# Identity products where TensorE waits, and VectorE work reordered, at the end of a fused attention before an expert-choice layer

## The reference, cut to what matters

```python
x = x + tanh(g_xattn) * xattn(layernorm(x), ctx, mask, Wq..bo)   # x: 2 x 2048 x 512, ctx: 2 x 77 x 512, one head
x = x + tanh(g_ffn) * ffn(layernorm(x), gate_w, w1, w2)

def ffn(x, gate_w, w1, w2):                 # 8 experts, w1 8 x 512 x 2048, w2 8 x 2048 x 512
    probs = softmax(einsum('ntd,ed->nte', x, gate_w))
    g, m = top_k(probs.transpose(0, 2, 1), 512)      # each expert takes 512 tokens of each batch
    h = gelu(einsum('nekd,edf->nekf', x[batch, m], w1))
    h = einsum('nekf,efd->nekd', h, w2)
    out[batch, m] += g * h
```

## Time and profile before

| | |
|---|---|
| median of 3 runs | 1557.32 us (1556.76 to 1558.54) |
| the profiled execution, its own time | 1556.92 us |
| its span | 1555.2 us |
| TensorE products busy | 1498.2 us, 96% |
| VectorE busy | 1016.6 us, 65% |
| ScalarE busy | 721.5 us, 46% |
| GpSimd busy | 589.4 us, 38% |
| granted TensorE clock, mean | 0.986 |

### The profile page before, as it was taken

The page is one execution under the profiler, slowest core; times in us unless marked ns, Lnnn a source line. Parts: engine busy times, 40 slices in busy tenths (PEclk is TensorE's granted clock), DMA queues, the critical chain, the costliest instruction groups (busy, mean ns, idle before and its releaser), DMA issues.

```text
span 1555.2 us, 20287 instructions
## 1 busy us (share of the span) xinstructions
PE 1498.2 (96%) x7329; PEld 1230.2 (79%) x7329; DVE 1016.6 (65%) x1714; ACT 721.5 (46%) x1270; POOL 589.4 (38%) x554
## 2 busy tenths in 40 slices
PE   6987699999999999999999999999999999999997
PEld 6765477787788888888888888888888888888886
DVE  2677676657766676676667666667667665766543
ACT  2244433355444554454445554554445444554432
POOL 2264555534544044323443244404432344323311
PEclk9998799999999999999999999999999999999999
DMA  7274623533342333344233423334324423342133
GB/s 230 76 242 158 203 89 118 135 127 85 86 123 58 105 88 102 95 88 116 82 109 73 117 78 113 66 97 101 96 89 88 116 81 109 79 111 73 49 71 79
DMA packets 101385, 163.37 MB, mean 105 GB/s; under 512 B 7411, under 2 KB 45315, under 8 KB 101285
## 3 DMA queue, kind: packets, MB, share of 16 engines
q1 hardware_dynamic: 86885, 128.50, 26.5%
q0 software_dynamic: 14400, 33.56, 11.5%
HBM read 128.48 MB, written 33.55 MB: 104 GB/s over the span
## 4 chain that ended last, share of the span: by engine, by line
PE 88%; DVE 7%; DMA 2%; issue 1%; ACT 1%; POOL 1%; SPq 0%; POOLq 0%; DVEq 0%; ACTq 0%
PE bank L1408 42%; PE bank L1294 33%; PE bank L1268 4%; PE bank L1585 2%; PE bank L565 1%; DVE atleast L971 1%; DVE onehot L1468 1%; DMA x_s<-in_x 1%; PE bank L406 1%; PE bank L589 1%; DVE x L840 1%; DVE hid_low L1286 0%; DMA ctx_raw<-in_ctx 0%; PE bank L1457 0%; PE bank L554 0%
## 5 line engine op out<-in xcount | busy, mean ns | idle before, releaser
L1408 PE MATMUL bank<-w2hl,hh 128*128 128x512 f32 x2024 | 628.8, 392 | 0.0
L1294 PE MATMUL bank<-xo,whl 128*128 128x512 f32 x2352 | 544.0, 390 | 3.5 <-DVE mix L1358 2.8
L1294 PEld LDWEIGHTS bank<-xo,whl 128*128 128x128 f32 x2352 | 442.0, 188 | 97.3 <-DVE mix L1358 3.7
L1408 PEld LDWEIGHTS bank<-w2hl,hh 128*128 128x128 f32 x2024 | 376.2, 188 | 75.3
L1408 PE MATMUL bank<-w2hl,hid_low 128*128 128x512 f32 x1012 | 394.0, 389 | 0.0
L1408 PEld LDWEIGHTS bank<-w2hl,hid_low 128*128 128x128 f32 x1012 | 190.1, 188 | 39.8
L1532 POOL DMA_INDIRECT layer_out<-y,slot_row x64 | 104.6, 1634 | 296.7 <-ACT y L1447 281.3
L1222 POOL TENSOR_TENSOR whl<-raw,whl 128x512 fp32r<-128x512 f32 x56 | 81.3, 1452 | 261.1 <-ACT whl L1188 261.1
L1253 DVE TENSOR_TENSOR w2hl<-raw,w2hl 128x512 fp32r<-128x512 f32 x213 | 147.8, 716 | 40.6 <-ACT w2hl L1248 40.6
L1248 ACT ACTIVATE w2hl<-raw 128x512 fp32r<-128x512 f32 x228 | 136.5, 624 | 58.9 <-DMA raw<-in_L_ffn_w 40.1
L1227 POOL TENSOR_TENSOR whl<-wsum,whl 128x512 fp32r<-128x512 f32 x56 | 73.9, 1319 | 183.5 <-ACT whl L1209 183.5
(11 more groups left out here) (230 smaller groups left out, 1792.1 us busy)
## 6 DMA issues: line engine op xcount, KB each, us to landing
raw<-in_L_ffn_w SPq DMA_DIRECT2D x228, 256.0 KB, 2.7
raw<-in_L_ffn_w SPq DMA_DIRECT2D x72, 512.0 KB, 4.9
x_s<-in_x SPq DMA_DIRECT2D x8, 1024.0 KB, 9.5
layer_out<-x SPq DMA_DIRECT2D x8, 1024.0 KB, 10.4
xn_rows<-xn SPq DMA_DIRECT2D x8, 1024.0 KB, 5.2
raw_k<-in_L_xattn_Wk SPq DMA_DIRECT2D x1, 1024.0 KB, 5.5
raw_q<-in_L_xattn_Wq SPq DMA_DIRECT2D x1, 1024.0 KB, 11.3
raw_v<-in_L_xattn_Wv SPq DMA_DIRECT2D x1, 1024.0 KB, 13.4
```

Of the source, the lines that this page charges most:

```text
L1294: last = pe.matmul(bk[:, :], whl[:, p % 2, part, 2 * w + k, :], xo[:, xpart, x, k, :], start=(not adds and k == 0 and part == HIGH and xpa ...
L1408: last = pe.matmul(Y_BANKS[c][:, :], high if hpart == HIGH else low[:, c * P:(c + 1) * P], w2hl[:, f % 4, part, :], start=(s == 0 and hpar ...
```

## The change

TensorE gets products of the identity with itself into a bank that holds nothing in use (`keep_running`): 16 ahead of `turn_e(7)`, 2 ahead of each of the four `tokens_pe`, 4 ahead of `hidden_pe(0, 0)`. The low part of the first pair of w1 moves from GpSimd, where it stood ahead of the gathers, to VectorE ahead of the token splits. On GpSimd the deviations of step 6 move ahead of the gathers. On VectorE the last two `logits_out` move ahead of the split of the fourth token block. TensorE's part of piece 0 of the second choice moves from `hidden_pe(0, 1)` into `output_pe(0, 0)`. At the end of expert 0 ScalarE's copy of the first product of expert 1 moves up by one block, ahead of the copies of two blocks of w2 and of the sums' high part, and VectorE's low parts of the first two blocks of w2 of expert 1 move from ahead of `combine_dve` to behind the output rows. `w1_low_pool` is renamed `w1_low_part`, and its call for the second pair waits for the first.

```diff
--- before.py
+++ after.py
@@ -589,6 +589,11 @@
             pe.matmul(O_BANKS[n % 2][:, :], eT[:, q % 2, i * P:(i + 1) * P], vo[:, q // QB, :],
                       start=True, stop=True).then_inc(weighed, 1)
 
+        def keep_running(pe, bk, n):
+
+            for _ in range(n):
+                pe.matmul(bk[:, 0:P], ident[:, :], ident[:, :], start=True, stop=True)
+
         def attention_pe(pe, between):
             wait_evacuated(pe, step_at["mean", 0])
             pe.wait_ge(tails, 2 * B)
@@ -603,6 +608,8 @@
                 if q + 1 < NQ:
                     for i in range(Q - 1):
                         score(pe, q + 1, i)
+                if q + 1 == NQ:
+                    keep_running(pe, SC_BANKS[0], 16)
                 turn_e(pe, q)
                 if q + 1 < NQ:
                     score(pe, q + 1, Q - 1)
@@ -766,14 +773,13 @@
                         rows(q, i)
 
 
-            w1_low_pool(pool, 0, 0, 0)
+            deviations(NQ - 2)
             for c in range(NC):
                 gather_pool(pool, 0, 0, c)
-            deviations(NQ - 2)
             deviations(NQ - 1)
             for f in range(2):
                 w2_low_sub(pool, 0, 0, f)
-            w1_low_pool(pool, 0, 0, 1)
+            w1_low_part(pool, 0, 0, 1)
             for q in (NQ - 2, NQ - 1):
                 for i in range(Q):
                     rows(q, i)
@@ -894,10 +900,12 @@
                     mean_out(q)
                 between(q, 3)
                 between(q, 4)
-            for c in range(NC):
+            w1_low_part(dve, 0, 0, 0)
+            for c in range(NC - 1):
                 split_tokens_dve(dve, 0, c)
             logits_out(NQ - 2)
             logits_out(NQ - 1)
+            split_tokens_dve(dve, 0, NC - 1)
 
         def attention_over(eng):
 
@@ -1208,7 +1216,10 @@
             act.wait_ge(w1_sums, pairs_before(e, p) * 3 + 3)
             act.activation(whl[:, p % 2, HIGH, 2 * S1:14, :], wsum[:, :, :], ACT.Copy).then_inc(w1_sum_high, 1)
 
-        def w1_low_pool(pool, e, b, p):
+        def w1_low_part(pool, e, b, p):
+
+            if is_plain(e) and b == 0 and p == 1:
+                pool.wait_ge(w1_low, 1)
             high, low = whl[:, p % 2, HIGH, :, :].bitcast(F32), whl[:, p % 2, LOW, :, :]
             pool.wait_ge(w1_high, pair_no(e, b, p) + 1)
             if is_plain(e):
@@ -1255,7 +1266,7 @@
 
 
 
-        def hidden_pe(pe, b, f, inside=None):
+        def hidden_pe(pe, b, f):
             n = step_no(0, b, f)
             p = f // 2
             if f == 0:
@@ -1269,8 +1280,6 @@
                                      xp[:, b, xpart, k, :],
                                      start=(k == 0 and part == HIGH and xpart == HIGH),
                                      stop=(k == KD - 1 and part == LOW))
-                if k == 1 and inside is not None:
-                    choice_pe(pe, 1, inside)
             last.then_inc(h_sum, 1)
 
         def gelu_act(act, b, f):
@@ -1630,7 +1639,7 @@
         OPERANDS_2 = {7: 0, 9: 1, 11: 2, 13: 3}
 
         def choice_piece(b, f):
-            return f if b == 0 and 1 <= f < N_PIECES else None
+            return f if b == 0 and f < N_PIECES else None
 
         def next_pair(b, f):
 
@@ -1653,7 +1662,7 @@
             for b in range(B):
                 for f in range(KF):
                     if f + 1 < KF:
-                        hidden_pe(pe, b, f + 1, 0 if b == 0 and f == 0 else None)
+                        hidden_pe(pe, b, f + 1)
                     if b == 0:
                         if f == SLOTS_1:
                             slots_pe(pe, 1)
@@ -1680,6 +1689,8 @@
                         operands_high_act(act, 1, OPERANDS_2[f])
                     if f % 2 == 0:
                         w1_high_act(act, *next_pair(b, f))
+                        if b == 1 and f + 2 == KF:
+                            copy_p1_act(act, 1, 0)
                         if next_pair(b, f)[0] == 1:
                             w1_sum_high_act(act, 1, next_pair(b, f)[2])
                     if b == 0 and f == LAST_SLOT:
@@ -1690,7 +1701,6 @@
                 if b == 0:
                     gelu_act(act, 1, 0)
                 else:
-                    copy_p1_act(act, 1, 0)
                     hidden_act(act, 1, 0)
                 for c in (0, 1):
                     output_rows(act, 0, b, c, y_act)
@@ -1698,7 +1708,7 @@
         def plain_dve(dve, own):
             for b in range(B):
                 for f in range(KF):
-                    if choice_piece(b, f) is not None:
+                    if f > 0 and choice_piece(b, f) is not None:
                         choice_dve(dve, own, 1, choice_piece(b, f))
                     if f + 1 < KF:
                         split_hidden_dve(dve, b, f + 1)
@@ -1707,7 +1717,8 @@
                     if b == 1 and f in OPERANDS_2:
                         operands_mix_dve(dve, 1, OPERANDS_2[f])
                     if b == 1:
-                        w2_low_sub(dve, *next_block(b, f))
+                        if next_block(b, f)[0] == 0:
+                            w2_low_sub(dve, *next_block(b, f))
                     else:
                         if f == HOT_1:
                             hot_dve(dve, 0, 1)
@@ -1731,6 +1742,9 @@
                     combine_dve(dve, 1, 0)
                 for c in (2, 3):
                     output_rows(dve, 0, b, c, y_dve)
+                if b == 1:
+                    for f in range(2):
+                        w2_low_sub(dve, 1, 0, f)
 
         def plain_pool(pool):
             for b in range(B):
@@ -1740,7 +1754,7 @@
                     if w2_no(*next_block(b, f)) < W2_EARLY:
                         w2_low_sub(pool, *next_block(b, f))
                     if f % 2 == 0:
-                        w1_low_pool(pool, *next_pair(b, f))
+                        w1_low_part(pool, *next_pair(b, f))
                     if b == 0 and f == GATHER_1:
                         for c in range(NC):
                             gather_pool(pool, 0, 1, c)
@@ -1869,7 +1883,7 @@
             for p in range(NP):
                 new = following_pair(e, p, final)
                 if new is not None:
-                    w1_low_pool(pool, new[0], 0, new[1])
+                    w1_low_part(pool, new[0], 0, new[1])
                 if p == 2:
                     promote_pool(pool, e, 1)
                 if p in GATHER_AT and not final:
@@ -2028,7 +2042,9 @@
             prep_pe(pe, 0)
             attention_pe(pe, beside_attention(first_choice_pe(pe)))
             for c in range(NC):
+                keep_running(pe, SC_BANKS[1], 2)
                 tokens_pe(pe, 0, c)
+            keep_running(pe, SC_BANKS[1], 4)
             hidden_pe(pe, 0, 0)
 
             pe.wait_ge(rinv_ready, NQ)
```

## The result

The changed kernel takes 1549.88 us, the median of 6 runs (1547.80 to 1553.91), beside 1557.87 us (1555.69 to 1558.56) for the kernel before on the same chip: ratio 0.9952, 95% interval 0.9937 to 0.9967. That is faster, inside the forecast range of 1544.0 to 1551.0 and 2.7 us above its 1547.2. The profiled execution is the quickest of the six: 1547.80 us, span 1545.7, against a forecast of 1546.8.

The account below looks back on a forecast made before the run. TensorE, busy nearly throughout, was taken as the bound, winnable only where it stands or runs at half clock. From 1556.92 us, 7.7 plus 2.4 us gave 1546.8 profiled, 1547.2 median; range 1544.0 to 1551.0.

Parts of the forecast that it names:

- The bound and the two places: TensorE bounds the kernel; time can be won only between 149 and 192 us and in expert 1's first pair.
- Integer operations, 1.8 us: With w1's low part off GpSimd, VectorE's two integer operations shorten and `turn_e(7)` comes 1.8 us earlier; bounds 0 and 2.0.
- Sixteen identity products, 4.3 us, full clock at even odds: Ahead of `turn_e(7)`: 32 instructions take 4.3 us inside a wait; even odds of full clock, worth 0.8 us in `route`.
- do not do what they are for: Rival, chance 0.12: `turn_e` and `route` stay at half clock, perhaps the last turn too; 1548.0 us.
- Deviations ahead of the gathers, first gather at 161.9: On GpSimd, the first gather waits for step 6's deviations and starts at 161.9 us, 2.0 us earlier than before.
- Gathers beside VectorE, +0.5 us: VectorE's w1 subtractions, at about 164.5 to 166 us, delay the third and fourth gathers by 0.5 us; bounds 0 and 1.6.
- Last turn, 0.5 us won, hidden products from 172.85: Identity products keep the clock at the last turn of tokens, saving 0.5 us; first hidden product at 172.85 us.
- The choice beside GpSimd, 8.4 us to the output block: Second choice, started at 172.8 us beside GpSimd's subtractions, takes 8.4 us instead of 6.49; bounds 6.0 and 10.5.
- Piece 0 behind the first quarter of the output block: The count is done before the gelu's split, so TensorE no longer waits; gain included in the choice's term.
- The end of expert 0, 2.4 us: Two waits in expert 1's first pair of 42 products go: gain up to 2.5 us, taken as 2.4.
- Slower, by 0.55 us an identity instruction: Rival, chance 0.03: instructions at 0.55 us give 1560.5 us; costs begin at 0.22, the sum is lost at about 0.53.
- The median lies 0.4 us above the profiled one: Step from the profiled forecast of 1546.8 us to the median forecast of 1547.2 us.

Follow-up runs that it names:

- the second set: The changed kernel measured again with no edit: median 1551.61 us, ratio to the kernel before 0.9949.
- the logits apart: Changed kernel plus identity products in the waits of steps 4 and 5, logits of step 6 ahead of the first token split: 1546.41 us, ratio 0.9923.

## Why the prediction was right, and where it was off

*The bound and the two places.* Right. All of the gain lies up to 192 us (7.6 us) and in the pair at 368 us (2.4 us); the trace ends 9.5 us earlier.

*Integer operations, 1.8 us.* Right, at the upper bound: from the first of them to the next operation it takes 0.28 us instead of 2.31, so 2.0 us are won. `turn_e(7)` comes 2.3 us earlier, since the first of them already started 0.3 us sooner, and 2.1 us go when the subtraction is put back.

*Sixteen identity products, 4.3 us, full clock at even odds.* The size was near: 32 instructions at 0.117 us, 3.7 us. The odds were not met. TensorE stood 3.1 us behind them, the turn (1.14 us) and `route` (1.87 us) ran at half clock; this is the rival "do not do what they are for" for its first half. It is not the same in every execution: in two other profiles with the same 16 products and the same wait (3.2 us) the turn ran at full clock (0.66 us) and `route` at half (1.88). At the last turn of tokens the clock was full (0.66 us). And what full clock would bring was mis-signed: I counted it as a small gain in every place, but in the one profile that kept it up to the gathers (26 products) the last tokens were 3.5 us later, by the turn. What I had not asked is what the faster products release: the store of 1024 KB, if the reading above holds. The 4 products ahead of the first hidden block did not keep the clock either: TensorE waited 2.4 us, the granted clock was 0.50 from 176 to 178 us, and the first 24 products took 7.4 us against 5.7 in other profiles; VectorE being later, that cost nothing. In all, the products that the change is named after are worth nothing that these runs can tell, with the rest of the change (0.9942 against 0.9952) or alone (1.0003).

*Deviations ahead of the gathers, first gather at 161.9.* Right: 161.75, released by them. With the gathers first they start about 0.15 us sooner at the same clock of the turn, and nothing comes of it.

*Gathers beside VectorE, +0.5 us.* Wrong in size, and in the changed kernel also in place: TensorE at half clock needed until 166.2 us for the values and VectorE until 167.0 for the rows, so the subtractions of w1 came at 167.12, behind the last gather. The trace of before could have told: there VectorE's last row of step 7 ended at 168.6 us, which less the 2.0 us forecast is 166.6, not 164.5.

```profile
167.84 0.75 DVE L840 SCALAR_TENSOR_TENSOR x<-bank,rinv,x_s 128x512 f32<-128x512 f32 x1 [0.36 <-PE bank L589]
```

Where they did lie beside gathers, as in the kernel with 26 products, these took 0.95 us and followed each other 1.25 us apart, as undisturbed. So nothing was added to the gather instructions by two operations of 128x512 of two float32 inputs; that their landing was late in the same profiles is the open point above. The Trainium skill (SBUF — State Buffer, Who interferes with whom) has it so, that such an operation was not seen to stall descriptor writing; here the traces agree, and what stretched the gather to 2.75 us stays open.

*Last turn, 0.5 us won, hidden products from 172.85.* The turn yes, the start no: 173.97. Of the six logits operations, which I gave 0.2 us each, the sixth met GpSimd's subtraction of w2 and took 1.23 us, and the last split waited behind it. I had placed GpSimd's start at 172.7; it began at 172.00, released by ScalarE's high part of w2. In six other profiles with this order all six were short; what the place of the logits of step 6 adds, no run shows.

*The choice beside GpSimd, 8.4 us to the output block.* The term that was mis-sized, and it hid the last one: from 172.8 to 181.2 as I put it, 173.83 to 181.17 in the trace, 7.3 us. The forecast added 1.9 us to the 6.49 of before: 0.7 for ScalarE and 1.2 for two operations. ScalarE had finished the high part of w1 at 173.31, before it was wanted, so the 0.7 was 0; of the operations `cand` was long (1.18 us, and 0.67 already before the change) and the one ahead of the exponential by 0.2 us. A late start met less of GpSimd, an early one more. Over the profiles with the changed order, the chain takes 8.6 to 8.9 us where the choice starts within 0.25 us of GpSimd's first subtraction (9.3 with TensorE's part in the hidden block), 8.2 where it starts 0.7 us behind it, and 7.3 to 7.6 where it is 1.8 to 3.1 us behind. So the two errors, +1.0 and -1.1, are largely one mechanism, and the third block at 184.07 stood 0.1 us from its forecast of 183.95. That they cancel so closely is luck; that they have opposite signs is not: GpSimd's two subtractions have to be sat out once, in the logits or in the choice.

*Piece 0 behind the first quarter of the output block.* Right that TensorE no longer waits, worth 0 at the start of the output block; if the piece stays in the hidden block, TensorE stands 3.2 us there and the output block behind it takes 1.3 us longer at the lower clock.

*The end of expert 0, 2.4 us.* Right to 0.1 us.

*Slower, by 0.55 us an identity instruction.* Excluded: 0.117 us. Its second threshold was also reckoned wrongly: a loss of 3.2 us at 0.55 us an instruction falls to nothing 0.1 us lower, at about 0.45 us, not 0.53.

*The median.* The sum, 1546.8 us, is 1.0 below the profiled execution. "The median lies 0.4 us above the profiled one", taken from the kernel before, is what failed: it lies 2.1 above, and the profiled execution of the second set lies 6.1 above its own median. The kernel's time depends on what clock TensorE is granted in places that the change doesn't touch: 0.50 or 0.92 in steps 5 and 6, which comes with a turn 6.9 us later in one profile; and one more, behind the third pair of expert 1. There TensorE waits 1.8 to 1.9 us in all fourteen profiles; behind it, twelve instructions take about 4.6 us in six of them, the kernel before and both profiles of the changed one among these, and about 3.18 in eight. The kernel with the logits apart, at the place of the row 396.86 above:

```profile
396.85 3.18 PE L1308 MATMUL bank<-xo,whl 128*128 128x512 f32 x12 [1.88 <-DVE mix L1372]
```

## What to carry to other kernels

Move a consumer's small operations out of the time in which another engine runs its long two-input ones, and check which operations then meet it instead: the logits gained about 5 us in the traces by their place (3 us in the medians), the identity products nothing by theirs. Filler products kept the clock where it is lost over many products (steps 4 to 6: the granted clock 1.00 in all three such profiles, runs within 2 to 4 us of each other, 2.5 to 10 without them); in front of a short turn that hangs on someone else they brought nothing. An engine that is done sooner and then stands can lose the gain again: output blocks behind a wait of 2.2 us or more took 3.0 to 5.5 us, the three without a wait 2.9. Before making a stretch faster, ask which large store it will release, and what small transfer that store may run ahead of; the traces here suggest such a case and do not prove it.

## What was not expected of the hardware

- A pause does not settle the clock. Behind the same wait of 1.8 to 1.9 us twelve instructions ran in about 3.2 or 4.6 us, whatever the kernel. Behind 16 identity products and a wait of 3.1 to 3.2 us the turn ran in 0.66 or in 1.14 us, and one program got 0.50 or 0.92 in the same 15 us in two executions.
- A float32 product of 128 columns costs two instructions of 0.115 to 0.117 us at full clock: 3.73 us for 32, 5.97 us for 52.
- Operations of 128x32 or 128x56 elements with two inputs take 0.2 us alone and 1.2 us beside a GpSimd subtraction of 128x512 (1.25 us each); two integer operations of one input, 128x128, 0.23 us instead of 1.2.
- The four gathers of 128 rows landed 3.6 to 4.4 us after their issue (median of the four) in eleven profiles, and 5.7 to 6.8 us after it in the three in which a store of 1024 KB was issued up to 0.8 us behind the start of the last one, or before it.
